# Spread decays in a buffer of their own and loaded a step ahead, convolution inputs in a rotation of three, products ahead of the dots

## The reference

```python
q = silu(dwconv(x @ Wq.T)); k = silu(dwconv(x @ Wk.T)) * DK**-0.5; v = silu(dwconv(x @ Wv.T))   # 4 causal taps
a = sigmoid(x @ Wa.T + ba); beta = sigmoid(x @ Wb.T + bb)
def step(S, inp):
    qt, kt, vt, at, bt = inp
    err = einsum('bhij,bhj->bhi', S, kt) - vt
    S = at[..., None] * S - bt[..., None, None] * (err[..., None] * kt[:, :, None, :])
    o = einsum('bhij,bhj->bhi', S, qt)
    return (S, o)
```

## Time and profile before

| | us |
|---|---|
| median of 2 runs | 7834.9 (7826.45 to 7843.36) |
| profiled execution: its time | 7857.47 |
| profiled execution: span | 7855.7 |
| DVE busy / PE busy / POOL busy / ACT busy | 5401.3 / 5058.1 / 3639.5 / 3259.9 |

### The profile page before, as it was taken

The page is one execution under the profiler, slowest core; times in us unless marked ns, Lnnn a source line. Parts: engine busy times, 40 slices in busy tenths (PEclk is TensorE's granted clock), DMA queues, the critical chain, the costliest instruction groups (busy, mean ns, idle before and its releaser), DMA issues. The chain is left out here.

```text
span 7855.7 us, 175713 instructions
## 1 busy us (share of the span) xinstructions
PE 5058.1 (64%) x58695; PEld 3316.1 (42%) x58695; DVE 5401.3 (69%) x16005; ACT 3259.9 (41%) x6914; POOL 3639.5 (46%) x4232
## 2 busy tenths in 40 slices
PE   5655556556556565565555652677777777777777
PEld 4544444444444444444444442333433333333333
DVE  6777777777777777777877775565655655656655
ACT  4444444434444343444443441344444444444444
POOL 3766667666676676766766665111111111111110
PEclk8777777777777777777777775788888888888888
DMA  4655556555565565655655554111111121111111
GB/s 113 145 130 143 132 135 145 129 141 141 130 146 133 133 144 121 149 133 135 149 133 131 133 132 110 41 44 40 43 41 40 41 51 47 50 42 40 44 41 34
DMA packets 1172906, 786.91 MB, mean 100 GB/s; under 512 B 1039923, under 2 KB 1091795, under 8 KB 1157844
## 3 DMA queue, kind: packets, MB, share of 16 engines
q1 hardware_dynamic: 864468, 583.96, 30.6%
q10 hardware_dynamic: 307712, 193.48, 10.3%
HBM read 473.80 MB, written 303.50 MB: 99 GB/s over the span
## 5 line engine op out<-in xcount | busy, mean ns | idle before, releaser
L457 POOL TENSOR_TENSOR qp<-qp,ab 128x512 f32<-128x512 f32 (+7 forms) x1024 | 1024.9, 1001 | 75.3
L462 POOL TENSOR_TENSOR qp<-qp,pt 128x512 f32<-128x512 f32 (+7 forms) x1024 | 935.0, 913 | 81.6 <-issue 1.4
L821 DVE SCALAR_TENSOR_TENSOR p_bank<-y,conv_w,p_bank 128x128 f32<-128x128 f32 x3072 | 827.9, 349 | 182.2 <-ACT p_bank L648 168.4
L1678 DVE TENSOR_REDUCE nmax<-w_bank 128x1 f32<-128x512 f32 x1024 | 638.3, 684 | 327.7 <-PE w_bank L1304 317.6
L1259 POOL TENSOR_TENSOR ot<-ot,ln_w 128x1024 f32<-128x1024 f32 x64 | 150.6, 2352 | 1422.6 <-ACT ot L1534 1422.6
L570 PE MATMUL f_bank<-vt,sc 32*32 32x64 f32 x8192 | 226.8, 302 | 865.0 <-DMA vt<-e_dram 858.2
L839 DVE TENSOR_TENSOR st<-d_bank,st 128x512 f32<-128x512 f32 x496 | 319.3, 686 | 587.9 <-PE d_bank L494 578.9
L459 POOL TENSOR_TENSOR pt<-qp,vb 128x512 f32<-128x512 f32 (+7 forms) x1024 | 704.5, 688 | 15.1 <-DVE vb L898 15.1
L570 PEld LDWEIGHTS f_bank<-vt,sc 32*32 32x32 f32 x8192 | 213.2, 165 | 895.7 <-issue 895.7
L590 PEld LDWEIGHTS p_bank<-xnT,wqkv 128*128 128x128 f32 x4096 | 520.8, 208 | 134.5 <-issue 134.5
L494 PE MATMUL d_bank<-xd,kt 32*64 32x128 f32 x7936 | 387.4, 350 | 285.3 <-DVE st L839 183.1
(11 more groups left out here) (219 smaller groups left out, 11663.5 us busy)
## 6 DMA issues: line engine op xcount, KB each, us to landing
decay_or_prod<-decay_dram SPq DMA_DIRECT2D x124, 1024.0 KB, 10.5
prod_dram<-decay_or_prod ACTq DMA_DIRECT2D x64, 1280.0 KB, 8.0
kp<-prod_dram SPq DMA_DIRECT2D x64, 640.0 KB, 6.9
qp<-prod_dram SPq DMA_DIRECT2D x64, 640.0 KB, 7.8
a_dram<-at ACTq DMA_DIRECT2D x64, 512.0 KB
ab<-a_dram SPq DMA_DIRECT2D x64, 512.0 KB, 14.8
v_dram<-vt ACTq DMA_DIRECT2D x64, 512.0 KB
vb<-v_dram SPq DMA_DIRECT2D x64, 512.0 KB, 3.9
```

What stands on the lines that cost most here:

```text
L457: link(nc.gpsimd.tensor_tensor(q, q, ab[:, g, r:r + 1, :].to_broadcast([128, w, DV]), ALU.mult), 1)
L462: link(nc.gpsimd.tensor_tensor(q, q, pt2[:, 0:w], ALU.add))
L821: nc.vector.scalar_tensor_tensor(out=zz, in0=y[:, m, :, tap:tap + C], scalar=conv_w[:, m, tap:tap + 1], in1=zz, op0=ALU.mult, op1=ALU.add) ...
L1678: nc.vector.tensor_reduce(nmax[:, n:n + 1], bank[:], AX.X, ALU.max, negate=True).then_inc(freed, 1)
```

## The change

The decays get a buffer of their own (`db`), and `prod` and `xo` share another. `y` holds three banks in rotation instead of six.

- **SP.** The two loads into `db` move from the head of the slot of s + 1 to the slot of s itself, behind the `xe` loads and ahead of the `xk` load; they wait for the write of the decays (`dec_wr`) and until the state of s - 1 has been decayed. The `vb` load moves from ahead of the `kp` load to behind the write of the update.
- **DVE.** `decay` moves from after tap group 11 to right behind the first half. The additions of `state` come after groups 9, 12, 14 and 16.
- **PE.** `update` pair 1 now goes ahead of `cross`; `products` goes ahead of `scores`.
- **ACT.** `crossed` no longer waits for `decayed`; it waits for the landing of the write of the products instead, and `products` waits for the landing of the `x_dram` write. `left` is gone: each `evict` first copies the old halo of its own bank to `y` and waits for that copy. `products` comes ahead of the last `silu` and of `masked_scores`.

```diff
-DECAY_AFTER_TAPS, STATE_AFTER_TAPS = 11, (11, 14, 15, 17)
+Y_BANKS = 3
+STATE_AFTER_TAPS = (9, 12, 14, 16)
...
-        y = sb("y", [128, MT, GB, TAPS - 1 + C])
+        y = sb("y", [128, Y_BANKS, 4, GB, TAPS - 1 + C])
...
-        decay_or_prod = sb("decay_or_prod", [128, GB * HP * DV])
-        db = decay_or_prod[:].rearrange("p (m i) -> p m i", i=DV)
-        prod = decay_or_prod[:, 0:GB * 4 * ROW].rearrange("p (b c) -> p b c", b=GB)
-        xo = decay_or_prod[:, GB * 4 * ROW:GB * 4 * ROW + HD]
+        db = sb("db", [128, GB * HP, DV])
+        prod = sb("prod", [128, GB, 4 * ROW])
+        xo = prod[:].rearrange("p b c -> p (b c)")[:, 0:HD]
...
-                if updates(lo - 1, hi - 1):
-
-                    sp.wait_ge(*dma_of(dec_wr, n, g, -1))
-                    held(sp, sp_passed)
-                    for par in range(2):
-                        rows = decay_dram[o][par:par + 1].to_broadcast([64, GB * HP, DV])
-                        sp.dma_start(db[64 * par:64 * par + 64], rows).then_inc(db_in[o], 16)
...
+                if updates(lo, hi):
+                    sp.wait_ge(*dma_of(dec_wr, n, g, 0))
+                    held(sp, sp_passed)
+                    if due(s):
+                        sp.wait_ge(decayed, s)
+                        held(sp, sp_passed)
+                    for par in range(2):
+                        rows = decay_dram[g][par:par + 1].to_broadcast([64, GB * HP, DV])
+                        sp.dma_start(db[64 * par:64 * par + 64], rows).then_inc(db_in[g], 16)
+                if valid(lo, hi):
                     sp.wait_ge(*dma_of(x_wr, n, g, 0))
...
-                    sp.wait_ge(*dma_of(v_wr, n, g, 1))
-                    held(sp, sp_passed)
-                    sp.dma_start(vb[:, o], v_dram[o].rearrange("t b h i -> (b h) t i")).then_inc(vb_in[o], 16)
...
                     sp.dma_start(upd_dram[g].rearrange("b h t i -> (b h) (t i)"), eb[:]).then_inc(upd_wr[g], 16)
                 if valid(lo + 1, hi + 1):
+                    sp.wait_ge(*dma_of(v_wr, n, g, 1))
+                    held(sp, sp_passed)
+                    sp.dma_start(vb[:, o], v_dram[o].rearrange("t b h i -> (b h) t i")).then_inc(vb_in[o], 16)
...
                 if ahead:
                     betas(s + 2, g)
+                if state:
+                    update(*before, (1,))
                 if valid(lo, hi):
                     cross(s, n, g)
                 if state:
-                    update(*before, (1, 2, 3))
+                    update(*before, (2, 3))
                 if front:
+                    products(s + 1, n + g, 1 - g)
                     scores(s + 1, 1 - g)
-                    products(s + 1, n + g, 1 - g)
                     front2(s + 1, n + g, 1 - g)
...
+                rows = y[:, j % Y_BANKS]
+                nc.scalar.activation(rows[:, :, :, 0:TAPS - 1], halo[:, g, 4 * j:4 * j + 4], ACT.Copy).then_inc(halo_done, 1)
+                act.wait_ge(halo_done, CONV_BANKS * s + j + 1)
                 nc.scalar.activation(halo[:, g, 4 * j:4 * j + 4], now[:, :, :, C - TAPS + 1:], ACT.Copy)
...
-                if state:
-                    act.wait_ge(decayed, s)
+                act.wait_ge(*dma_of(p_wr, n, g, 0))
...
+                    act.wait_ge(*dma_of(x_wr, n, g, -1))
...
                     silu(s + 1, 1 - g, 4)
+                    products(s + 1, n + g, 1 - g)
+                    silu(s + 1, 1 - g, 5)
                     masked_scores(s + 1, 1 - g)
-                    silu(s + 1, 1 - g, 5)
-                    products(s + 1, n + g, 1 - g)
...
                 if now:
                     half(s, n, g, 0)
+                if update:
+                    decay(s - 1, n - 1 + g, 1 - g)
...
-                    if k == DECAY_AFTER_TAPS and update:
-                        decay(s - 1, n - 1 + g, 1 - g)
```

More of the change, by code:

```diff
@@ L698, in masked_scores, with crossed @@
                     last.then_inc(f_freed, 1)
-            def crossed(s, n, g, state):
-                if state:
-                    act.wait_ge(decayed, s)
+            def crossed(s, n, g):
+                act.wait_ge(*dma_of(p_wr, n, g, 0))
                 if due(dma_of(x_wr, n, g, -1)[1]):
@@ L714, in products @@
             def products(s, n, g):
-                if due(dma_of(p_wr, n, g, -1)[1]):
+                if due(dma_of(x_wr, n, g, -1)[1]):
                     act.wait_ge(*dma_of(p_wr, n, g, -1))
+                    act.wait_ge(*dma_of(x_wr, n, g, -1))
                 for b in range(GB):
@@ L724, in products @@
                     act.wait_ge(*dma_of(kp_in, n, g, -2))
-                act.dma_start(prod_dram[g].rearrange("m p c -> p m c"), prod.rearrange("p b (q c) -> p (b q) c", c=ROW)).then_inc(p_wr[g], 16)
-            def left(s, g):
-                if due(CONV_BANKS * s):
-                    act.wait_ge(silu_done, CONV_BANKS * s)
-                nc.scalar.activation(y[:, :, :, 0:TAPS - 1], halo[:, g], ACT.Copy).then_inc(halo_done, 1)
-                act.wait_ge(halo_done, s + 1)
+                act.dma_start(prod_dram[g].rearrange("m p c -> p m c"), prod[:].rearrange("p b (q c) -> p (b q) c", c=ROW)).then_inc(p_wr[g], 16)
             def transposed(s, g):
@@ L777, in slot @@
                 if valid(lo, hi):
-                    crossed(s, n, g, state)
+                    crossed(s, n, g)
                 if front:
                     silu(s + 1, 1 - g, 4)
+                    products(s + 1, n + g, 1 - g)
+                    silu(s + 1, 1 - g, 5)
                     masked_scores(s + 1, 1 - g)
-                    silu(s + 1, 1 - g, 5)
-                    products(s + 1, n + g, 1 - g)
                     front2(s + 1, n + g, 1 - g)
                 if ahead:
-                    left(s + 2, g)
                     for j in range(2):
@@ L821, in conv @@
                     nc.vector.scalar_tensor_tensor(
-                        out=zz, in0=y[:, m, :, tap:tap + C], scalar=conv_w[:, m, tap:tap + 1], in1=zz,
+                        out=zz, in0=y[:, j % Y_BANKS, i, :, tap:tap + C], scalar=conv_w[:, m, tap:tap + 1], in1=zz,
                         op0=ALU.mult, op1=ALU.add).then_inc(conv_chain, 1)
```

2 lines of the change are left out of this document (1 added, 1 removed).

## The result

The changed kernel takes 7635.4 us (7630.1 to 7640.6), 0.9745 of the kernel before, with an interval of 0.9692 to 0.9799: 2.5% faster, 200 us, where 595 us and a time of 7240 (7040 to 7460) were forecast. The span of the profiled execution fell from 7855.7 to 7628.3 us. 209 of these 227 us lie ahead of the last decay, whose start moved from 4748.3 to 4539.4.

The account below looks back on a forecast made before the run. VectorE with its waits, 14.2 us a step, was taken to bound the kernel. A step from 62.35 to 53.0 us saves 9.35 us, times 62 steps 580 us: 7277, less 22.6 gives 7255, predicted as 7240 (7040 to 7460).

Parts of the forecast that it names:

- E: Moment when a step's first half ends; the next first half was forecast at E + 53.0 instead of E + 62.35.
- The overlap of decays and `x_dram` write: Ahead of the second half: decays under way delay the x_dram write, bounds nothing to 5.4 us, taken as 1.5 us.
- From the last additions to the convolution: Stretch up to the first convolution: 20.9 us before, forecast 23.1, so the convolution starts at E + 42.9.
- the step from E to the last additions: After the first half: pair 1, then cross at E + 9.4; last additions end at E + 19.8 instead of E + 31.3.
- My first rival: Decays in the way of the x_dram write: second half at E + 30.5, gain 6.2 us a step, 7450; chance 0.16.
- the term of `vb`: Ahead of the next first half: vb behind kp and update's write costs 0 to 2 us, scaled at about E + 52.0.
- the gain of an early update's write: After the second half: L379 issued at once, not 7.4 us later, bringing xd and GpSimd's next start forward.
- the order of products: After the last additions: scores and its eviction now precede front2, making it 0.6 to 2.6 us later, taken as 2.5.
- the crowd ahead of the first half: Rival: vb, kp and update crowd the queue, costing 3 us more; gain 6.5 us a step, 7430; chance 0.1.
- The clock: Rival between the halves: shorter idling keeps TensorE at 2.4 GHz, saving 3 to 4 us more, 7030; chance 0.12.
- The other side's rival: L326's stall on SP stays, write still at E + 10.8; step 74 to 77 us, 7835 to 7990 us; chance 0.08.

Follow-up runs that it names:

- e11: Changed kernel with scores ahead of products, decays loaded in 4 KB pieces and the a_dram write issued behind the x_dram write; 0.9361 of the kernel before.
- e3: Changed kernel with the same spread decays loaded by eight DMAs of 4 KB a partition instead of two of 16 KB; 0.9654 of the kernel before.
- e4: Changed kernel with only one of the two decay loads, half the bytes, results not those of the reference; 0.9511 of the kernel before.
- e7: e1 with the two decay loads moved behind the loads of xk and x; 0.9730 of the kernel before.
- e10: Changed kernel with the vb load ahead of the kp load and the update's write again; 0.9569 of the kernel before.
- e1: Changed kernel with scores and its eviction ahead of products again, on TensorE and ScalarE; 0.9527 of the kernel before.

## Why the prediction was wrong

**Right.** VectorE and its waits bound the step. SP was held in the issue of `ab` by the decays ahead of it, and the move frees it: the write at E + 0.2. The decay's wait is gone. The overlap of decays and `x_dram` write costs the second half little: 7.2 us from the write's issue to `xk` instead of 6.2, 1.0 us, where I took 1.5. From the last additions to the convolution 23.2 us against 23.1, and to the values' write 18.9 against 18.8. Both of these are right by luck, with two errors that cancel. The step that I read took 16.6 us to the values' write with the dots ahead, where the mean over the steps is 15.1, and the dots behind cost 3.9 us, not 2.2. To the convolution it took 20.9 us, where the mean is 20.0, and the change added 3.2 us, not 2.2.

**Wrong, the step from E to the last additions: `cross` starts at E + 9.4, the additions end at E + 19.8.** Measured: E + 11.6 and E + 24.9. This step holds 5.1 of the 6.1 us.

- The start of `cross`, 2.2 us late. Pair 1 takes 1.98 us, not 1.5. In one kind of step it stands behind the betas, which wait for late gates; in the other the gates' write is issued among the `xe` loads, which land 3 us late. I had costed the order on TensorE but not what stands ahead of the moved pair. e11 takes the second kind away: 1.0%.
- `cross` and the pairs themselves. I used their durations of before, when the decays were through before TensorE came to these matmuls. In their new place the decays hold up the loading of TensorE's own instructions: issue waits 3.4 us a step instead of 1.1. e3, e4 and e7 show it. e4 puts 2.25 us a step on half of the transfer, and with the decays elsewhere (e7) the additions end at E + 21.3, within 1.5 us of the forecast. My first rival had the decays in the way at this very place, and priced only the `x_dram` write.

**Mis-sized, the term of `vb`.** I gave its new place 0 to 2 us and let it fit, or set the step by a microsecond. It cost 1.3 us in the write (8.8 instead of 7.5 us from its issue to the `vb` load), and with that `vb` became the last link. Undone, it is worth 1.7 us a step (e10). I had seen the gain of an early update's write, but the next first half does not wait for GpSimd's start or for `xd`, so nothing came of it.

**Mis-sized, the order of products.** My own sum had it as a loss of 2.5 us. Undone it is worth 1.9 us a step (e1), and 3.9 us on its own piece of the chain.

**Left out, the first half.** I took the work before E as unchanged. It grew from 12.05 to 12.7 us, 0.6 us a step, mostly in L922; its cause is open.

**Wrong, the range.** Each rival was priced alone, at 7430 to 7450. Two of them came together, and they add up, since one lies ahead of the last additions and the other behind. The first came by another mechanism than I gave it: the decays were in the way of TensorE's instructions, while the `x_dram` write lost only 1.0 us. The second, the crowd ahead of the first half, came at less than its 3 us. The clock gave nothing back. The stretch from E to the second half of the step above (columns as in the earlier trace rows):

```profile
2379.54:2409.00 29.46, 16.17 (x313) 13.99 (x316) 21.23 (x58) 10.61 (x19) 17.06 (x20) 0.56 0.57 140
```

0.56 of the full clock against 0.55, still almost always the level of 1.2 GHz; TensorE is busy 16.17 of 29.46 us there, and idles 5.44 us in one piece. The other side's rival, a stall that stays on SP, did not happen.

## What to carry to other kernels

A transfer that no engine waits for still has a price: ask what else runs on the DMA engines in its new place, and count the engines' own instructions among it, above all beside long runs of small matmuls. Before giving one operation the lead over another on a chain, ask whether the one behind was running in a wait that will now be idle; the dots cost much less there. When several moves each look harmless, add their upper bounds along the chain, as those ahead of a joint and behind it add up.

## What the hardware showed that was not expected

- Instruction packets hardly start while the decays run (10 of them from 20 to 28 us of the step over all steps, against 75 in e7, and 52 in the 4 us behind), and TensorE idles up to 8.2 us. With packets of 4 KB in place of 16 KB in the way its waits fall from 3.4 to 1.9 us a step, with the same bytes in no less time.
- Padding each 256-byte row of the target by 8 bytes turned 16 KB packets into packets of 4096 bytes, not of 256, and these took 0.41 us each, where those of an unpadded load took 0.29. A write on the other queue took 3 us longer beside them.
- One row of 16 KB sent to many partitions passes at about 13 bytes a ns on each DMA engine, `kp`'s load of 5 KB rows at 26 (196 ns a packet). Neither 16 rows as sources nor 128 partitions in one load changed this; loads of 16 partitions each made it 8. Why is open.
- An issue on ScalarE's queue in the middle of SP's eight `xe` loads made one of these issues take 2.5 us instead of 0.3; with that issue moved away (e11) none of them takes over 0.8 us.
